# Head attention of a graph network on one core: loops written out, TensorE's steps regrouped in twos, a weight ring of six, VectorE's masks one slot later

## The chip, the cores and the metric

One core of one Trainium2 chip (trn2) runs the whole kernel. The metric is the device time of one execution in microseconds (us); lower is better. The kernel before takes 3810.34 us, the median of three runs.

## The reference, cut to what matters

Four layers work on `x` (8 batches, 2048 nodes, 128 features) with one adjacency matrix `adj` (2048 x 2048): an additive attention, the head attention that is changed here, a neighbour mean, and another additive attention. The change touches layer 1 only, and of it the part between the projections and the output product:

```python
h = maximum(layernorm(x), 0)
q = (h @ W_q).reshape(8, 2048, 4, 32).transpose(0, 2, 1, 3)   # k and v alike
scores = einsum('bhnd,bhmd->bhnm', q, k) / sqrt(32)
scores = where(adj == 0, -inf, scores)
attn = softmax(scores, axis=-1)
out = einsum('bhnm,bhmd->bhnd', attn, v)
x = x + out.transpose(0, 2, 1, 3).reshape(8, 2048, 128) @ W_o + b_o
```

So there are 8 x 4 softmaxes over 2048 x 2048 masked scores.

## The kernel before, in words

`build` runs the stages one after the other, each a block of five engine programs. `nodes1` leaves q and k (float16, a high and a low part) and v in memory, `head_attention` (lines 1046 to 1330) leaves the weighted sums and their denominators, `nodes2` divides and goes on.

`head_attention` treats the four heads of a batch as two units `u` of two heads `a`. A **chunk** is one unit and 512 query nodes (`BANK`), so a batch has `CHUNKS` = 8 and the stage has 64. A **step** `g` is one tile of 128 key nodes (`jt`, 16 of them) of a chunk, for both heads: 128 steps a batch (`BODY`), 1024 in all. In a step:

- **scores**: TensorE makes two matmuls (97 x 128 by 97 x 512, L1231), one for each head, into the two banks of `sc_ps` (`SB` = 2). Row 96 of `qs` holds minus the row's maximum (the "shift"), so no score can overflow. The second head's scores of step g use the bank that the second head's exponential of step g - 1 reads.
- **exponential**: ScalarE, L1314, one instruction for each head, into slot `g % PB` of the ring `w` (`PB` = 4).
- **mask**: `w` is multiplied by 0 or 1 in place: by GpSimd (L1327) in three steps of four, by VectorE (L1276, `mask`) in the steps with `g % 4 == 1` (`mine`).
- **sums**: `weigh(g - LAG)`, with `LAG` = 3: two float32 matmuls (128 x 33 by 128 x 512, L1205) that add into `o_ps`. The profile shows each as two passes, so a step of sums is 4 matmuls.

The shift of a chunk must be known before its scores. So two chunks ahead TensorE also computes plain scores of the same rows with the high parts only, as **slots**: a chunk has 16 of them, one a step (`slot`, L1189), each a pair of 32-row matmuls of the two heads. They go to a ring `mx_ps` of `MB` = 2 slots, and VectorE reads each with two instructions (L1263: add the mask's bias, take the maximum). A slot may be written only when VectorE has taken the one two before it:

```python
pe.wait_ge(mx_taken, SLOTS * chunk + k + 1)      # mx_taken starts at MB + 1
```

After the 16th slot VectorE reduces the maxima (L1270). In step 4 of the next chunk a seventeenth slot, TensorE's transpose of these maxima (L1184), is taken by VectorE (L1252), and SyncE carries the result through memory into row 96 of `qs` (`place_shift`).

An engine executes in program order, and what orders the engines is a set of counting semaphores. TensorE's order in a step is slot, scores, scores, sums of three steps before. Step 4 has the transpose ahead of its scores and its own slot behind its sums. VectorE's order is the mask of step g - 1 where there is one, then the slot of step g.

The batches are a hardware loop (`Fori(0, B)`) in each of the five programs. At a body's end TensorE runs the three sums that are still due, ScalarE copies the last rows out (`keep_rows`), and SyncE has issued loads for a following batch, in the last round too (batch 0 again, `following`). The slots of "two chunks ahead" are run in the last round as well, and nobody uses them.

Of the kernel before, what the change touches and what calls it, by code (L numbers as in the profile page):

```python
# [18 lines left out]
B = 8  # L19
N = 2048  # L20
F = 128
T = N // P
# [1016 lines left out]
def head_attention(nc, io, keep):  # L1039
# [17 lines left out]
    PB, LAG = 4, 3  # L1057
    SB, MB = 2, 2
    mine = [g for g in range(BODY) if g % 4 == 1]
    with ExitStack() as stack:  # L1060
# [50 lines left out]

        def ring(k, chunk_parity):

            return (k + chunk_parity) % MB
# [13 lines left out]
        @block.sync  # L1128
        def _(sp):
            load(sp, 0, 0)  # L1130
            for t in range(T):
                sp.dma_start(mbias[:, t, :], io["mask_bias"][t * P:(t + 1) * P, :]).then_inc(
                    mbias_early if t < 2 * RT else mbias_loaded, 16)
            load_v(sp, 0, 0)
            load(sp, 0, 1)
            load_v(sp, 0, 1)
            place_shift(sp, 0, 0, 0)

            def store(b, c):

                sp.wait_ge(o_kept, 2 * CH * b + c + 1 + 2)
                u, rows = c // CH, slice(c % CH * BANK, (c % CH + 1) * BANK)
                for a in range(2):
                    head = 2 * u + a
                    sp.dma_start(io["heads_t"][bass.ds(b, 1), head * HD:(head + 1) * HD, rows].rearrange("one p n -> p (one n)"),
                                 oe[2 * HD * a:2 * HD * a + HD, c % 2, :]).then_inc(o_stored[c % 2], 16)
                    sp.dma_start(io["sums"][bass.ds(b, 1), head:head + 1, rows].rearrange("one p n -> p (one n)"),
                                 oe[2 * HD * a + HD:2 * HD * a + HD + 1, c % 2, :]).then_inc(o_stored[c % 2], 16)

            with sp.Fori(0, B) as b:  # L1150
                following = (b + 1) % B
                for c in range(CHUNKS):
                    if c == CH:
                        sp.wait_ge(scored, 2 * (BODY * b + STEPS))
                        load(sp, following, 0)
                    if c >= 1:
                        store(b, c - 1)
                    place_shift(sp, CHUNKS * b + c + 1, (c + 1) % CHUNKS // CH, (c + 1) % CH)
                    if c == CH:
                        sp.wait_ge(weighed, BODY * b + STEPS + PB)  # L1160
                        load_v(sp, following, 0)
                sp.wait_ge(scored, 2 * BODY * (b + 1))
                load(sp, following, 1)
                store(b, CHUNKS - 1)
                sp.wait_ge(weighed, BODY * (b + 1) + PB)
                load_v(sp, following, 1)
            for u in range(2):
                sp.wait_ge(qk_loaded[u], LOADS * (B + 1))
                sp.wait_ge(v_loaded[u], 16 * (B + 1))
                sp.wait_ge(o_stored[u], 64 * CH * B)  # L1170
            sp.wait_ge(shift_placed, 32 * (CHUNKS * B + 1))

        @block.tensor
        def _(pe):
            def slot(k, chunk, u, c, first=False):

                n, buf = slots(first)[k], ring(k, c % 2)
                if n < 0 and first:
                    return
# [13 lines left out]
            def weigh(g, i):  # L1193
# [10 lines left out]
                for a in range(2):  # L1204
                    mm = nc.tensor.matmul(o_ps[2 * HD * a:2 * HD * a + HD + 1, c % 2, :], v[u][:, jt, a, :], w[:, g % PB, a, :],  # L1205
                                          start=(jt == 0), stop=(jt == T - 1))
# [9 lines left out]
            with pe.Fori(0, B) as i:  # L1216
                for g in range(BODY):
# [3 lines left out]
                    if jt == 0 and tc == 0:  # L1221
                        pe.wait_ge(qk_loaded[tu], LOADS * (i + on + 1))
                    mine_now = of_step(jt)
                    slot(mine_now[0], CHUNKS * i + g // T + 2, tu, tc)
# [9 lines left out]
                    if g >= LAG:  # L1234
                        weigh(g - LAG, i)
                    for k in mine_now[1:]:
                        slot(k, CHUNKS * i + g // T + 2, tu, tc)
                for g in range(BODY - LAG, BODY):
                    weigh(g, i)

        @block.vector
        def _(dve):
            def slot(k, chunk, c, parity, masks, first=False):

                n, buf = slots(first)[k], ring(k, c % 2)
                if n < 0 and first:
                    return
# [8 lines left out]
                else:  # L1256
                    if not isinstance(due, int):
                        dve.compute_val(due)
# [13 lines left out]
            def mask(g, i):  # L1272
                if g in mine:
                    c, jt = g // T % CH, g % T
                    dve.wait_ge(exp_done, 2 * (BODY * i + g + 1) + SB)
                    nc.vector.tensor_tensor(w[:, g % PB], w[:, g % PB],  # L1276
# [10 lines left out]
            with dve.Fori(0, B) as i:  # L1287
                for g in range(BODY):
                    if g >= 1:
                        mask(g - 1, i)  # L1290
                    for k in of_step(g % T):
                        slot(k, CHUNKS * i + g // T + 2, target(g // T)[2], g // T % 2, (mbias_loaded, 16 * (T - 2 * RT)))
                mask(BODY - 1, i)

        @block.scalar
        def _(act):
# [11 lines left out]
            with act.Fori(0, B) as i:  # L1308
                for g in range(BODY):
                    act.wait_ge(weighed, BODY * i + g + 1)  # L1310
                    for a in range(2):
                        n = 2 * g + a
                        act.wait_ge(scored, 2 * BODY * i + n + 1)
                        nc.scalar.activation(w[:, g % PB, a], sc_ps[:, n % SB], ACT.Exp, scale=SCALE).then_inc(exp_done, 1)  # L1314
                    if g >= T + LAG and (g - LAG) % T == 0:
                        keep_rows((g - LAG) // T - 1, i)
                keep_rows(2 * CH - 1, i)

        @block.gpsimd
        def _(pool):  # L1320
            with pool.Fori(0, B) as i:
                for g in range(BODY):
# [4 lines left out]
                    nc.gpsimd.tensor_tensor(w[:, g % PB], w[:, g % PB],  # L1327
# [653 lines left out]
```

## Time and profile before

| | |
|---|---|
| time, median of 3 runs (lowest, highest) | 3810.34 us (3809.37, 3810.83) |
| the profiled execution's own time | 3810.15 us |
| its span, first to last instruction | 3808.4 us |
| TensorE busy over the span | 3485.4 us (92%) |
| VectorE, ScalarE, GpSimd busy | 3143.4, 1725.5, 1775.2 us |
| mean granted TensorE clock | 0.948 |
| scores of head attention, first to last start | 926.7 to 2869.2 us |

The span lies 1.75 us under the time of the same execution. Times in the rows below are microseconds from the span's start, so they can be laid against each other between engines. TensorE's matmuls are pipelined and their ends are modelled, so the gaps between starts tell what a matmul costs, not the durations.

### The profile page before, as it was taken

The numbers are of one execution on the slowest core, as the hardware profiler recorded it, in microseconds if no ns is written. First come the engines' busy times: TensorE is split into PE (matmuls) and PEld (weight loads), VectorE is DVE, ScalarE is ACT, GpSimd is POOL, SyncE is SP. The second block draws the span as 40 slices with busy tenths as digits, with TensorE's granted clock in tenths as the row PEclk, the third lists the DMA queues.
The fourth block names the chain that finished last, engine by engine and source line by source line (L and its number), as shares of the span: only waits on it lengthen the run. The fifth ranks groups of instructions, "written<-read, shape, count | busy, mean of one in ns | idle before, by whom it ended". The sixth has DMA issues, their size and how long they took to land. (4 is left out here: it accounts for less than half of the span.)

```text
span 3808.4 us, 69809 instructions
## 1 busy us (share of the span) xinstructions
PE 3485.4 (92%) x21189; PEld 1824.9 (48%) x21204; DVE 3143.4 (83%) x7168; ACT 1725.5 (45%) x3546; POOL 1775.2 (47%) x828
## 2 busy tenths in 40 slices
PE   5769999674999999999999999999996999699999
PEld 4659999550111111111111111111114999599999
DVE  6768888667998989989899899898996776477777
ACT  7811111361665656656556566565662544210100
POOL 2300000111887878878888888887882111000000
PEclk8779999895999999999999999999997999899999
DMA  6422121264001110111001110111003332221220
GB/s 238 176 106 79 58 84 57 110 235 157 9 25 28 29 28 5 28 28 28 24 10 29 28 28 6 28 28 28 22 13 109 115 112 79 84 85 51 84 77 36
DMA packets 61261, 245.77 MB, mean 65 GB/s; under 512 B 12130, under 2 KB 14564, under 8 KB 46692
## 3 DMA queue, kind: packets, MB, share of 16 engines
q1 hardware_dynamic: 60900, 241.14, 18.5%
q8 instruction: 204, 3.34, 0.4%
q14 instruction: 157, 1.29, 0.1%
HBM read 156.03 MB, written 85.07 MB: 63 GB/s over the span
## 5 line engine op out<-in xcount | busy, mean ns | idle before, releaser
L1327 POOL TENSOR_TENSOR a_w<-a_w,keep_mask_t 128x1024 f32<-128x1024 f32 x768 | 1635.5, 2155 | 406.1 <-ACT a_w L1314 406.1
L1263 DVE CUSTOM_DVE_ANT_0 a_mx_ps<-a_mx_ps,a_mbias 128x512 f32<-128x512 f32 x2112 | 1389.6, 719 | 143.0 <-PE a_mx_ps L1189 128.8
L1314 ACT ACTIVATE a_w<-a_sc_ps 128x512 f32<-128x512 f32 x2048 | 1111.4, 595 | 813.9 <-PE a_sc_ps L1231 812.5
L1205 PE MATMUL a_o_ps<-a_w,a_v 128*33 128x512 f32 x4096 | 1084.7, 609 | 5.7 <-POOL a_w L1327 5.7
L839 PE MATMUL g_acc<-g_hv,g_w 128*128 128x129 f32 x8192 | 923.8, 276 | 37.0 <-DVE g_w L776 24.5
L839 PEld LDWEIGHTS g_acc<-g_hv,g_w 128*128 128x128 f32 x8192 | 922.3, 193 | 38.7 <-DVE g_w L776 38.7
L776 DVE SCALAR_TENSOR_TENSOR g_w<-g_row,keep_s,keep_mask_t 128x1024 f32<-128x1024 f32 x512 | 647.2, 1282 | 203.5 <-PE g_acc L839 183.6
L1231 PE MATMUL a_sc_ps<-a_qs,a_ks 97*128 97x512 f16 x2048 | 635.2, 393 | 0.0
L1189 PEld LDWEIGHTS a_mx_ps<-a_ks,a_qs 32*128 32x128 f16 x2112 | 94.8, 91 | 895.1 <-DVE a_mx L1263 467.9
L1189 PE MATMUL a_mx_ps<-a_ks,a_qs 32*128 32x512 f16 x2112 | 411.8, 397 | 76.7 <-DVE a_mx L1263 34.2
L1276 DVE TENSOR_TENSOR a_w<-a_w,keep_mask_t 128x1024 f32<-128x1024 f32 x256 | 459.9, 1796 | 1.0
L1205 PEld LDWEIGHTS a_o_ps<-a_w,a_v 128*33 128x33 f32 x4096 | 151.4, 109 | 449.2 <-issue 288.2
L1263 DVE DVE_READ_ACCUMULATOR2_ANT a_mx<- 128x1 f32 x2112 | 289.0, 137 | 0.0
L101 POOL TENSOR_TENSOR p_rstd<-p_tmp,p_minus_half 128x16 f32<-128x16 f32 x24 | 69.6, 2899 | 468.3 <-DVE p_tmp L88 468.3
L1820 PE MATMUL p_sum_ps<-p_g,keep_mask_t 128*128 128x256 f16 x2048 | 243.3, 274 | 1.4 <-issue 1.0
L1231 PEld LDWEIGHTS a_sc_ps<-a_qs,a_ks 97*128 97x128 f16 x2048 | 125.9, 98 | 241.8 <-issue 202.2
L919 POOL MEMSET p_minus_half<- 128x16 f32 x1 | 0.1, 117 | 493.0 <-POOLq L664 493.0
L1820 PEld LDWEIGHTS p_sum_ps<-p_g,keep_mask_t 128*128 128x128 bf16 x2048 | 201.2, 98 | 28.5 <-issue 1.3
L794 ACT COPY g_value<-keep_s 128x16 f32 (+1 forms) x16 | 3.3, 204 | 435.8 <-DMA g_h<-h_nodes 435.8
L803 ACT ACTIVATE g_e<-g_y 128x1024 f32<-128x1024 f32 x16 | 16.9, 1058 | 329.5 <-DVE g_y L741 329.5
L1537 DVE SCALAR_TENSOR_TENSOR p_x<-p_sum_ps,keep_rdeg,p_own 128x128 f32<-128x128 f32 x128 | 44.4, 347 | 72.2 <-PE p_sum_ps L1820 71.6
L1303 ACT COPY a_oe<-a_o_ps 33x512 f32<-33x512 f32 x128 | 73.6, 575 | 29.6 <-PE a_o_ps L1205 28.8
(198 smaller groups left out, 2130.4 us busy)
## 6 DMA issues: line engine op xcount, KB each, us to landing
h_nodes<-p_h SPq DMA_DIRECT2D x16, 1032.0 KB, 3.9
g_h<-h_nodes SPq DMA_DIRECT2D x16, 1032.0 KB, 6.0
p_adj_in<-in_adj SPq DMA_DIRECT2D x16, 1024.0 KB, 8.5
g_row<-u_rows SPq DMA_DIRECT2D x32, 512.0 KB, 7.2
p_x<-x SPq DMA_DIRECT2D x16, 1024.0 KB, 8.5
a_v<-v SPq DMA_DIRECT2D x18, 528.0 KB, 3.8
a_ks<-k_hi SPq DMA_DIRECT2D x72, 128.0 KB, 2.8
a_qs<-q_hi SPq DMA_DIRECT2D x72, 128.0 KB, 2.9
```

What stands on the lines that cost most here:

```text
L101: nc.gpsimd.tensor_tensor(rstd, tmp[:, 3, :], minus_half, ALU.pow).then_inc(rooted, 1)
L776: nc.vector.scalar_tensor_tensor(out=w[:, g % PB, :], in0=row[:, k, cols], scalar=keep["s2_08"][:, bass.ds(b, 1), jt], in1=keep["mask_t"][ ...
L839: mm = nc.tensor.matmul(tile(half, it), w[:, g % PB, it * P:(it + 1) * P], hv[:, k, jt, :], start=(jt == 0 and it % 3 == 0), stop=(jt == T ...
L1189: mm = nc.tensor.matmul(mx_ps[:, buf, a, :], qs[u][a][hi, t * P:(t + 1) * P], ks[u][a][hi, kc * BANK:(kc + 1) * BANK], start=True, stop=True)
L1205: mm = nc.tensor.matmul(o_ps[2 * HD * a:2 * HD * a + HD + 1, c % 2, :], v[u][:, jt, a, :], w[:, g % PB, a, :], start=(jt == 0), stop=(jt = ...
L1231: nc.tensor.matmul(sc_ps[:, n % SB, :], ks[u][a][:, jt * P:(jt + 1) * P], qs[u][a][:, c * BANK:(c + 1) * BANK], start=True, stop=True).the ...
L1263: last = nc.vector.tensor_tensor_reduce(out=mx_ps[:, buf, a, :], in0=mx_ps[:, buf, a, :], in1=mbias[:, t, kc * BANK:(kc + 1) * BANK], scal ...
L1276: nc.vector.tensor_tensor(w[:, g % PB], w[:, g % PB], keep["mask_t"][:, jt, c * BANK:(c + 1) * BANK].unsqueeze(1).to_broadcast([P, 2, BANK ...
L1303: ins = nc.scalar.copy(oe[rows, c % 2, :], o_ps[rows, c % 2, :])
L1314: nc.scalar.activation(w[:, g % PB, a], sc_ps[:, n % SB], ACT.Exp, scale=SCALE).then_inc(exp_done, 1)
L1327: nc.gpsimd.tensor_tensor(w[:, g % PB], w[:, g % PB], keep["mask_t"][:, jt, c * BANK:(c + 1) * BANK].unsqueeze(1).to_broadcast([P, 2, BANK ...
L1820: mm = nc.tensor.matmul(sum_ps[:, it % 2, 0:2 * F], keep["mask_t"][:, jt, it * P:(it + 1) * P], g[k][:, jt].rearrange("p two f -> p (two f ...
```

## The change

- `PB` goes from 4 to 6, and the ring's index counts over all steps, `(BODY * i + g) % PB`, since 128 is no multiple of 6.
- The loop over batches becomes a Python loop in all five programs. The sums due at a body's end are carried into the next batch, as is the last `keep_rows` and the last `store`.
- TensorE handles two steps at a time: for an even g the two slots of g and g + 1, the scores of g, the sums of g - 4 and g - 3, and then the scores of g + 1. In the round that starts at step 4 the transpose and one slot come first, and the third slot stands behind the sums (`late`).
- VectorE takes the slot of step g first and then the mask of g - 1.
- SyncE no longer loads batch 0 again at the end, and `wanted` leaves out the slots beyond the last chunk.

```diff
@@ -1054,7 +1054,7 @@
     UNITS = RT * CH
     TURN = UNITS // 4
     SLOTS = UNITS + 1
-    PB, LAG = 4, 3
+    PB, LAG = 6, 3
     SB, MB = 2, 2
     mine = [g for g in range(BODY) if g % 4 == 1]
     with ExitStack() as stack:
@@ -1109,6 +1109,12 @@
 
             return [k for k, n in enumerate(slots(False)) if (TURN if n < 0 else n) == jt]
 
+        def wanted(n, chunk):
+            return chunk < CHUNKS * B or chunk == CHUNKS * B and n in (-1, *range(TURN))
         def ring(k, chunk_parity):
 
             return (k + chunk_parity) % MB
@@ -1147,35 +1153,36 @@
                     sp.dma_start(io["sums"][bass.ds(b, 1), head:head + 1, rows].rearrange("one p n -> p (one n)"),
                                  oe[2 * HD * a + HD:2 * HD * a + HD + 1, c % 2, :]).then_inc(o_stored[c % 2], 16)
 
-            with sp.Fori(0, B) as b:
-                following = (b + 1) % B
+            for b in range(B):
+                more = b < B - 1
                 for c in range(CHUNKS):
-                    if c == CH:
+                    if c == CH and more:
                         sp.wait_ge(scored, 2 * (BODY * b + STEPS))
-                        load(sp, following, 0)
+                        load(sp, b + 1, 0)
                     if c >= 1:
                         store(b, c - 1)
-                    place_shift(sp, CHUNKS * b + c + 1, (c + 1) % CHUNKS // CH, (c + 1) % CH)
-                    if c == CH:
+                    elif b > 0:
+                        store(b - 1, CHUNKS - 1)
+                        sp.wait_ge(weighed, BODY * b + PB)
+                        load_v(sp, b, 1)
+                    if more or c < CHUNKS - 1:
+                        place_shift(sp, CHUNKS * b + c + 1, (c + 1) % CHUNKS // CH, (c + 1) % CH)
+                    if c == CH and more:
                         sp.wait_ge(weighed, BODY * b + STEPS + PB)
-                        load_v(sp, following, 0)
-                sp.wait_ge(scored, 2 * BODY * (b + 1))
-                load(sp, following, 1)
-                store(b, CHUNKS - 1)
-                sp.wait_ge(weighed, BODY * (b + 1) + PB)
-                load_v(sp, following, 1)
+                        load_v(sp, b + 1, 0)
+                if more:
+                    sp.wait_ge(scored, 2 * BODY * (b + 1))
+                    load(sp, b + 1, 1)
+            store(B - 1, CHUNKS - 1)
             for u in range(2):
-                sp.wait_ge(qk_loaded[u], LOADS * (B + 1))
-                sp.wait_ge(v_loaded[u], 16 * (B + 1))
                 sp.wait_ge(o_stored[u], 64 * CH * B)
-            sp.wait_ge(shift_placed, 32 * (CHUNKS * B + 1))
 
         @block.tensor
         def _(pe):
             def slot(k, chunk, u, c, first=False):
 
                 n, buf = slots(first)[k], ring(k, c % 2)
-                if n < 0 and first:
+                if n < 0 and first or not wanted(n, chunk):
                     return
                 if n < 0:
                     pe.wait_ge(rows_done, chunk)
@@ -1202,7 +1209,7 @@
                 else:
                     pe.wait_ge(masked_pool, (BODY - len(mine)) * i + g - sum(m < g for m in mine) + 1)
                 for a in range(2):
-                    mm = nc.tensor.matmul(o_ps[2 * HD * a:2 * HD * a + HD + 1, c % 2, :], v[u][:, jt, a, :], w[:, g % PB, a, :],
+                    mm = nc.tensor.matmul(o_ps[2 * HD * a:2 * HD * a + HD + 1, c % 2, :], v[u][:, jt, a, :], w[:, (BODY * i + g) % PB, a, :],
                                           start=(jt == 0), stop=(jt == T - 1))
                 mm.then_inc(weighed, 1)
 
@@ -1213,15 +1220,20 @@
                 for k in range(SLOTS):
                     slot(k, chunk, 0, chunk, chunk == 0)
             pe.wait_ge(units_ready, 4)
-            with pe.Fori(0, B) as i:
+            for i in range(B):
                 for g in range(BODY):
                     u, r = g // STEPS, g % STEPS
                     c, jt = r // T, r % T
                     on, tu, tc = target(g // T)
-                    if jt == 0 and tc == 0:
+                    chunk = CHUNKS * i + g // T + 2
+                    if jt == 0 and tc == 0 and chunk < CHUNKS * B:
                         pe.wait_ge(qk_loaded[tu], LOADS * (i + on + 1))
-                    mine_now = of_step(jt)
-                    slot(mine_now[0], CHUNKS * i + g // T + 2, tu, tc)
+                    late = []
+                    if g % 2 == 0:
+                        due = of_step(jt) + of_step(jt + 1)
+                        for k in due[0:2]:
+                            slot(k, chunk, tu, tc)
+                        late = due[2:]
                     if jt == 0:
                         pe.wait_ge(shift_placed, 32 * (CHUNKS * i + g // T + 1))
                     for a in range(2):
@@ -1231,19 +1243,21 @@
                         nc.tensor.matmul(sc_ps[:, n % SB, :], ks[u][a][:, jt * P:(jt + 1) * P],
                                          qs[u][a][:, c * BANK:(c + 1) * BANK], start=True, stop=True).then_inc(scored, 1)
 
-                    if g >= LAG:
-                        weigh(g - LAG, i)
-                    for k in mine_now[1:]:
-                        slot(k, CHUNKS * i + g // T + 2, tu, tc)
-                for g in range(BODY - LAG, BODY):
-                    weigh(g, i)
+                    if g % 2 == 0:
+                        for n in (BODY * i + g - 4, BODY * i + g - 3):
+                            if n >= 0:
+                                weigh(n % BODY, n // BODY)
+                        for k in late:
+                            slot(k, chunk, tu, tc)
+            for g in range(BODY - 4, BODY):
+                weigh(g, B - 1)
 
         @block.vector
         def _(dve):
             def slot(k, chunk, c, parity, masks, first=False):
 
                 n, buf = slots(first)[k], ring(k, c % 2)
-                if n < 0 and first:
+                if n < 0 and first or not wanted(n, chunk):
                     return
                 due = SLOTS * chunk + k + 1
                 if n < 0:
@@ -1254,8 +1268,6 @@
                     dve.wait_ge(shift_ready, chunk)
                     dve.sem_inc(mx_taken, 1)
                 else:
-                    if not isinstance(due, int):
-                        dve.compute_val(due)
                     dve.wait_ge(*masks)
                     dve.wait_ge(mx_scored, due)
                     t, kc = RT * c + n // CH, n % CH
@@ -1273,7 +1285,7 @@
                 if g in mine:
                     c, jt = g // T % CH, g % T
                     dve.wait_ge(exp_done, 2 * (BODY * i + g + 1) + SB)
-                    nc.vector.tensor_tensor(w[:, g % PB], w[:, g % PB],
+                    nc.vector.tensor_tensor(w[:, (BODY * i + g) % PB], w[:, (BODY * i + g) % PB],
                                             keep["mask_t"][:, jt, c * BANK:(c + 1) * BANK].unsqueeze(1).to_broadcast([P, 2, BANK]),
                                             ALU.mult).then_inc(masked_dve, 1)
 
@@ -1284,12 +1296,12 @@
             for chunk in range(2):
                 for k in range(SLOTS):
                     slot(k, chunk, chunk, chunk, (mbias_early, 16 * 2 * RT), chunk == 0)
-            with dve.Fori(0, B) as i:
+            for i in range(B):
                 for g in range(BODY):
+                    for k in of_step(g % T):
+                        slot(k, CHUNKS * i + g // T + 2, target(g // T)[2], g // T % 2, (mbias_loaded, 16 * (T - 2 * RT)))
                     if g >= 1:
                         mask(g - 1, i)
-                    for k in of_step(g % T):
-                        slot(k, CHUNKS * i + g // T + 2, target(g // T)[2], g // T % 2, (mbias_loaded, 16 * (T - 2 * RT)))
                 mask(BODY - 1, i)
 
         @block.scalar
@@ -1305,26 +1317,28 @@
 
             act.sem_inc(exp_done, SB)
             act.sem_inc(o_kept, 2)
-            with act.Fori(0, B) as i:
+            for i in range(B):
                 for g in range(BODY):
                     act.wait_ge(weighed, BODY * i + g + 1)
                     for a in range(2):
                         n = 2 * g + a
                         act.wait_ge(scored, 2 * BODY * i + n + 1)
-                        nc.scalar.activation(w[:, g % PB, a], sc_ps[:, n % SB], ACT.Exp, scale=SCALE).then_inc(exp_done, 1)
+                        nc.scalar.activation(w[:, (BODY * i + g) % PB, a], sc_ps[:, n % SB], ACT.Exp, scale=SCALE).then_inc(exp_done, 1)
                     if g >= T + LAG and (g - LAG) % T == 0:
                         keep_rows((g - LAG) // T - 1, i)
-                keep_rows(2 * CH - 1, i)
+                    if g == LAG and i > 0:
+                        keep_rows(2 * CH - 1, i - 1)
+            keep_rows(2 * CH - 1, B - 1)
 
         @block.gpsimd
         def _(pool):
-            with pool.Fori(0, B) as i:
+            for i in range(B):
                 for g in range(BODY):
                     if g in mine:
                         continue
                     c, jt = g // T % CH, g % T
                     pool.wait_ge(exp_done, 2 * (BODY * i + g + 1) + SB)
-                    nc.gpsimd.tensor_tensor(w[:, g % PB], w[:, g % PB],
+                    nc.gpsimd.tensor_tensor(w[:, (BODY * i + g) % PB], w[:, (BODY * i + g) % PB],
                                             keep["mask_t"][:, jt, c * BANK:(c + 1) * BANK].unsqueeze(1).to_broadcast([P, 2, BANK]),
                                             ALU.mult).then_inc(masked_pool, 1)
 
```

## Rows read from the trace of the kernel before

**Rows 1.** Windows: busy time of each engine, granted clock, DMA share, GB/s.
```profile
1164.14:1170.95 6.81, 3.07 (x15) 0.49 (x11) 0.82 (x3) 1.16 (x2) 2.13 (x2) 0.82 0.82 235
1170.95:1201.25 30.30, 30.06 (x119) 5.65 (x118) 27.65 (x68) 17.36 (x32) 23.62 (x11) 0.87 0.08 23
1500.00:1529.46 29.46, 29.46 (x131) 5.68 (x131) 28.23 (x71) 18.40 (x35) 25.52 (x13) 1.00 0.02 6
```

**Rows 2.** Tile a_sc_ps: count, duration ns min/median/max, first and last start.
```profile
L1231 PE MATMUL a_sc_ps<-a_qs,a_ks x2048: 377/381/634, 926.7 to 2869.2; 97*128 97x512 f16 x187
```

**Rows 3.** Timeline of a plain step: start, duration, engine, line, operation, count.
```profile
1502.70 0.39 PE L1189 MATMUL a_mx_ps<-a_ks,a_qs 32*128 32x512 f16 x2
1502.77 6.30 POOL L1327 TENSOR_TENSOR a_w<-a_w,keep_mask_t 128x1024 f32<-128x1024 f32 x3 [0.97 <-ACT a_w L1314]
...
1503.02 0.60 PE L1231 MATMUL a_sc_ps<-a_qs,a_ks 97*128 97x512 f16 x2
...
1503.45 1.09 ACT L1314 ACTIVATE a_w<-a_sc_ps 128x512 f32<-128x512 f32 x2 [0.76 <-PE a_sc_ps L1231]
...
1503.56 1.05 PE L1205 MATMUL a_o_ps<-a_w,a_v 128*33 128x512 f32 x4
...
1504.55 0.39 PE L1189 MATMUL a_mx_ps<-a_ks,a_qs 32*128 32x512 f16 x2
```

**Rows 4.** Timelines of GpSimd and TensorE at a batch's end.
```profile
1162.05 4.22 POOL L1327 TENSOR_TENSOR a_w<-a_w,keep_mask_t 128x1024 f32<-128x1024 f32 x2 [0.97 <-ACT a_w L1314]
...
1162.31 0.60 PE L1231 MATMUL a_sc_ps<-a_qs,a_ks 97*128 97x512 f16 x2
1162.84 2.77 PE L1205 MATMUL a_o_ps<-a_w,a_v 128*33 128x512 f32 x12
1166.33 1.05 PE L1205 MATMUL a_o_ps<-a_w,a_v 128*33 128x512 f32 x4 [0.72 <-POOL a_w L1327]
1170.41 0.61 PE L1189 MATMUL a_mx_ps<-a_ks,a_qs 32*128 32x512 f16 x2 [3.02 <-issue]
1170.95 1.03 PE L1231 MATMUL a_sc_ps<-a_qs,a_ks 97*128 97x512 f16 x2
1171.91 0.61 PE L1189 MATMUL a_mx_ps<-a_ks,a_qs 32*128 32x512 f16 x2
```

**Rows 5.** Timeline after a transpose: two slots in a row, VectorE idle before them.
```profile
1513.53 0.60 PE L1189 MATMUL a_mx_ps<-a_ks,a_qs 32*128 32x512 f16 x4
1514.07 0.60 PE L1231 MATMUL a_sc_ps<-a_qs,a_ks 97*128 97x512 f16 x2
1514.07 0.70 DVE L1263 CUSTOM_DVE_ANT_0 a_mx_ps<-a_mx_ps,a_mbias 128x512 f32<-128x512 f32 x1 [1.17 <-PE a_mx_ps L1189]
```

**Rows 6.** Timeline ahead of the steps: TensorE waits for VectorE's slots.
```profile
886.47 0.73 DVE L1263 CUSTOM_DVE_ANT_0 a_mx_ps<-a_mx_ps,a_mbias 128x512 f32<-128x512 f32 x1
887.12 0.73 DVE L1263 CUSTOM_DVE_ANT_0 a_mx_ps<-a_mx_ps,a_mbias 128x512 f32<-128x512 f32 x1
887.32 0.61 PE L1189 MATMUL a_mx_ps<-a_ks,a_qs 32*128 32x512 f16 x2 [0.69 <-DVE a_mx L1263]
```

**Rows 7.** Timelines of VectorE and GpSimd around two masks of VectorE.
```profile
1506.94 2.13 POOL L1327 TENSOR_TENSOR a_w<-a_w,keep_mask_t 128x1024 f32<-128x1024 f32 x1
1508.30 1.85 DVE L1276 TENSOR_TENSOR a_w<-a_w,keep_mask_t 128x1024 f32<-128x1024 f32 x1
...
1516.63 1.22 DVE L1276 TENSOR_TENSOR a_w<-a_w,keep_mask_t 128x1024 f32<-128x1024 f32 x1
1517.50 2.34 POOL L1327 TENSOR_TENSOR a_w<-a_w,keep_mask_t 128x1024 f32<-128x1024 f32 x1 [1.06 <-ACT a_w L1314]
1517.77 0.69 DVE L1263 CUSTOM_DVE_ANT_0 a_mx_ps<-a_mx_ps,a_mbias 128x512 f32<-128x512 f32 x1
```

**Rows 8.** Timeline of SyncE at the stage's end.
```profile
2877.39 0.37 SPq L1095 DMA_DIRECT2D a_v<-v  x1
```

## The prediction

> **What bounds the kernel now.** I read the windows first, then the tile of the scores, then the timeline of single steps. Head attention is half of the time: its scores start from 926.7 to 2869.2 us [rows 2]. A chunk of 16 steps takes 29.46 us with TensorE busy throughout and the clock at full speed [rows 1], so 1.84 us a step. The timeline says of what: from slot to scores 0.32, from scores to sums 0.54, from sums to the next slot 0.98 to 0.99 [rows 3]. No wait lies between these, so TensorE sets the pace. VectorE is busy 28.23 of 29.46 us, GpSimd 25.52: both are close behind.
>
> GpSimd and VectorE are tied together. A mask of VectorE that has GpSimd to itself at first takes 1.22 us. One that starts 1.36 us into an operation of GpSimd takes 1.85: GpSimd's ends at 1509.07 and the mask at 1510.15, 1.08 later. And GpSimd's operation that starts inside a mask takes 2.34 for 2.13, ending 1.99 us after the mask [rows 7]. So whoever comes second does its work after the other. The Trainium skill states this as a rule (SBUF — State Buffer, section SBUF: two separate sides): the pair of ports is an exclusive lock, held for a whole instruction by whoever starts first. By that rule, the trace agrees; it would matter most for a mask that starts just behind a GpSimd operation, which is a rival below.
>
> At a batch's end the rhythm breaks: scores at 1162.31, then again at 1170.95 [rows 4], 8.64 us for 1.84, and the next chunk takes 30.30 us at a mean clock of 0.87 [rows 1].
>
> **The loops written out.** The scores' starts cover 1942.3 us for 1023 steps [rows 2]; at 1.841 these would be 1883.6. Of the excess of 58.7, seven batch ends take 7 x 6.80 = 47.6, and 11.1 is left for the eight starts, 1.4 each. The change keeps one start: 57.3 us go. Within a batch the 128 steps are already straight code and run without a gap, so I expect no new cost from more of it. If code loading ate the whole gain, the sum would lack 57; if it costs nothing, it stands. I take nothing.
>
> **What TensorE would save.** Two slots in a row and the scores after them take 0.54 [rows 5] where two single ones take 0.64. A step of sums takes 0.98 alone; three steps in a row have 12 passes in 2.77 against 4 in 1.05 [rows 3, 4], so 0.86 for each further step, and two take 1.84. A round of two steps is then pair 0.54, scores 0.54, sums 1.84, scores and the change to the slots. The last is in no row: between 0.45 (as if the change were free, twice 0.23 from the x2 forms) and 0.63 (a change twice as dear as scores to sums). I take 0.54 as from scores to sums. That makes 3.46 for 3.68, or 27.7 us a chunk, if nothing waits.
>
> **What waits.** The ring of slots still has two places, and now both are written together. The second slot of a round, B, needs VectorE to be done with B of the round before, while the slots that VectorE could do meanwhile are not there yet. Prices for VectorE: it starts a slot 0.54 after TensorE does (1513.53, 1514.07) [rows 5]; its two instructions start 0.65 apart, so a slot is 1.30; TensorE writes the next 0.85 after the slot's second instruction started (886.47, 887.32) [rows 6]; a free mask holds it 1.14 (1516.63, 1517.77) [rows 7].
>
> Let 0 be the start of slot A in a round with g = 4k + 2, in which VectorE's new order is A, mask, B. VectorE starts A at 0.54 and the mask at 1.84. That mask is of step 4k + 1, whose scores started at -0.54; its exponentials start 0.43 later and take 1.09 [rows 3], so it is ready at 0.98. B starts at 2.98, its second instruction at 3.63, and TensorE may write B of the following round at 4.48. TensorE comes there at 3.46 + 0.23 = 3.69, so it waits about 0.8 us (some 0.3 less, since scores of the round at 0 already wait a little for exponentials, which changes nothing in this chain). Everything behind it waits too: from B to scores 0.31, to sums 0.54, to the odd scores 1.84, to the next A 0.54, together 3.23. The next A at g = 4k + 6 stands at 7.71. VectorE has done its two slots by 4.28 + 2.60 = 6.88 and idles until 8.25. So four steps take 7.71 instead of 7.36: TensorE's 3.23 and VectorE's 4.48 now follow one another instead of overlapping, and the wait costs more than the grouping saves.
>
> Is the mask free? In this frame the second head's scores of step 4k + 2 wait for the exponential that ends at 0.98, start at 1.04, and its own exponential ends at 2.07 (0.43 and 0.60 later). GpSimd's next mask starts there at the earliest; VectorE's starts at 1.84, ahead of it. GpSimd's three then run behind it: 2.91 to 4.90 (the 1.99 above), to 7.0 and to 9.1, and VectorE's next mask starts at 7.71 + 1.84 = 9.55. It is free by 0.2 on one side and 0.4 on the other, so I take 1.14.
>
> **The round with the transpose.** Its pair is the transpose and a slot; the third slot goes behind the sums. With x the time at which the pair's second is written: scores x + 0.31, sums x + 0.85, late slot x + 2.69, odd scores x + 3.00, next A x + 3.54. VectorE gets the late slot at x + 3.23 and is done at x + 4.53, later than A could start (x + 4.08). Then A 1.30, mask 1.14, B's first 0.65, release 0.85: x + 8.47. So 0.76 more than 7.71, once a chunk.
>
> A chunk: 3 x 7.71 + 8.47 = 31.60 us for 29.46. Over 64 chunks +137 us.
>
> **The rest.** The skipped slots: in the last two chunks rounds run without slots. There the second head's scores wait for an exponential: 0.43 + 1.09 + 0.06 (GpSimd's end at 1166.27 to TensorE's start at 1166.33 [rows 4] as such a delay) = 1.58, sums 0.31 later, 1.84 for them: 3.73 a round, 29.8 a chunk, so about 3 us less in all. SyncE ends the stage with a load of v issued at 2877.39 [rows 8], behind stores that alone will be left: 1.5 us less (at least 0.5, at most 4, from the loads ahead of them). The ring of six: step g's exponential needs the sums of g - 6, which lie in the round before, so it never waits; with four places it would. The last copy of a batch and its store move to step 3 of the next one. Behind them on SyncE stand a load of v for the second unit and the shift of chunk 1, which is needed 10 steps later: hidden behind some 19 us; without this cover its few us would fall on TensorE eight times. On ScalarE the copies still lie between exponentials as in every other chunk. GpSimd's masks are used a round later than before; by the frame above the third ends at 9.1 and its sums are due after 12.
>
> Sum, from the profiled execution's 3810.15 (0.2 under the median of the runs): + 137 - 57.3 - 3 - 1.5 = 3885 us.
>
> **Rivals.**
> 1. Faster: B's wait doesn't bind. The place is TensorE's wait for VectorE in the rounds without a mask. For it: VectorE's work for four steps, 4 x 1.30 + 1.14 = 6.34, is under TensorE's 6.92, so only the order is against it. Then GpSimd's lockstep with the masks is the floor: three operations 6.30 [rows 3] and 1.08 for the mask, less 0.14 of overlap, 7.24 for four steps, 29.0 a chunk: -30 - 62 gives 3719; at the old 29.46 it is 3748. It decides at a chunk of 30.43, where 64 x 0.97 equals the 62 gained elsewhere, that is at a period of 7.42: 0.29 less than my 7.71, in a chain of nine terms of which one is assumed. Against it: the other eight are read.
> 2. The mask loses the race to GpSimd. It starts 0.2 us ahead; if GpSimd's operation were first, the mask would end at 2.07 + 2.12 + 1.08 = 5.27, the period become 2.2 longer, 9.9, and the time about 4450. By the skill's rule above the same: the loser waits for the whole operation. It decides where the mask starts later than GpSimd's operation. If only some chunks lose it, the time is in between.
> 3. The grouping does what I say and unrolling gives nothing back, because straight code has to be fetched: 3885 + 57 = 3942.
> 4. TensorE's waits of 0.8 us in 7.7 lower its clock. At the lower level (1.2 GHz) slot to scores takes 0.54 and scores to slot 0.96 [rows 4]; with sums at twice their time a round is about 6.5, and the stage over 1000 us longer. Against it: where it fell, at a batch's end, TensorE had stood still for 3.02 us [rows 4]; the gaps to come are a quarter of that.
>
> **How the numbers follow.** My forecast has 0.72, with a range of its own of 3850 to 3925: the unread change from scores to slots gives 0.09 x 4 x 64 = 23 each way, and 0.05 in the handovers of the chain 13 more. Rival 1 has 0.12, rival 2 0.06, rival 3 0.04, rival 4 0.02; 0.04 is for a wait that binds in part only and ends near the old time. The range of 3825 to 3955 holds my case nearly whole, rival 3, and part of the last. Faster by over 0.2% (7.6 us, about what a measurement of this kernel can tell from no change) 0.13, within it 0.03, slower 0.84.
>
> **What the profile after would show.** No gaps at 1164 to 1171 or their like; chunks of 31.6 us; TensorE idle before L1189 in every second round, released by VectorE, 0.5 to 0.8 us, and VectorE idle about 1.4 us every four steps, released by TensorE; all masks of VectorE near 1.22 us. Two sums in a row at 1.84, and the odd scores to the slot at 0.54. I am wrong if chunks stay under 30.4 us, or if masks of over 3 us appear.

## The result and the profile after

The changed kernel takes 3873.3 us (median of 4 runs, 3871.8 to 3880.7) against 3810.6 before, a ratio of 1.0166 with a 95% interval of 1.0149 to 1.0184: 63 us slower. Forecast were 3885, 3825 to 3955. Its profiled execution took 3873.6 us.

The windows view of the kernel after: a chunk that holds a batch's end, the one behind it, and a plain one (columns as in [rows 1]).

```profile
1148.62:1180.27 31.65, 29.49 (x132) 6.80 (x131) 26.50 (x71) 18.47 (x35) 27.61 (x14) 1.00 0.03 7
1180.27:1211.65 31.38, 29.40 (x130) 6.67 (x130) 26.00 (x71) 18.32 (x34) 27.11 (x13) 1.00 0.26 71
1499.00:1530.40 31.40, 29.41 (x131) 6.77 (x129) 26.25 (x71) 18.40 (x36) 27.37 (x12) 1.00 0.02 5
```

A plain chunk takes 31.40 us for the 29.46 of [rows 1], and now TensorE has 2 us without work in it and VectorE 5. The end of a batch costs 0.25 us where it cost 6.8. The clock stays at 1.00 through the waits.

The timelines of TensorE and VectorE over four steps of the kernel after, from one slot A behind which a mask stands to the next such one (VectorE's next wait is its last line):

```profile
1521.16 0.60 PE L1196 MATMUL a_mx_ps<-a_ks,a_qs 32*128 32x512 f16 x4
1521.76 0.88 PE L1243 MATMUL a_sc_ps<-a_qs,a_ks 97*128 97x512 f16 x2
1522.57 1.91 PE L1212 MATMUL a_o_ps<-a_w,a_v 128*33 128x512 f32 x8
1524.41 0.60 PE L1243 MATMUL a_sc_ps<-a_qs,a_ks 97*128 97x512 f16 x2
1524.95 0.39 PE L1196 MATMUL a_mx_ps<-a_ks,a_qs 32*128 32x512 f16 x2
1525.56 0.39 PE L1196 MATMUL a_mx_ps<-a_ks,a_qs 32*128 32x512 f16 x2 [0.22 <-DVE a_mx L1275]
1525.88 0.61 PE L1243 MATMUL a_sc_ps<-a_qs,a_ks 97*128 97x512 f16 x2
1526.41 1.91 PE L1212 MATMUL a_o_ps<-a_w,a_v 128*33 128x512 f32 x8
1528.26 0.61 PE L1243 MATMUL a_sc_ps<-a_qs,a_ks 97*128 97x512 f16 x2
1528.80 0.60 PE L1196 MATMUL a_mx_ps<-a_ks,a_qs 32*128 32x512 f16 x4
```

```profile
1521.70 0.70 DVE L1275 CUSTOM_DVE_ANT_0 a_mx_ps<-a_mx_ps,a_mbias 128x512 f32<-128x512 f32 x1 [1.14 <-PE a_mx_ps L1196]
1522.32 0.73 DVE L1275 CUSTOM_DVE_ANT_0 a_mx_ps<-a_mx_ps,a_mbias 128x512 f32<-128x512 f32 x1
1522.96 1.22 DVE L1288 TENSOR_TENSOR a_w<-a_w,keep_mask_t 128x1024 f32<-128x1024 f32 x1
1524.10 0.69 DVE L1275 CUSTOM_DVE_ANT_0 a_mx_ps<-a_mx_ps,a_mbias 128x512 f32<-128x512 f32 x1
1524.71 0.73 DVE L1275 CUSTOM_DVE_ANT_0 a_mx_ps<-a_mx_ps,a_mbias 128x512 f32<-128x512 f32 x1
1529.34 0.70 DVE L1275 CUSTOM_DVE_ANT_0 a_mx_ps<-a_mx_ps,a_mbias 128x512 f32<-128x512 f32 x1 [0.98 <-PE a_mx_ps L1196]
```

From 1521.16 to 1528.80 are 7.64 us for four steps. Read the chain across the two engines: slot A written at 1521.16, VectorE at it at 1521.70, the mask at 1522.96, slot B at 1524.10 and 1524.71, and only then, 0.85 later, TensorE's B at 1525.56. TensorE had written the A before it at 1524.95 and could have gone on 0.23 later, so it waited 0.38. Then 3.24 to the next A at 1528.80, for which VectorE has idled 0.98; before the A at 1521.16 it had idled 1.14. I had put about 1.4.

### The profile page after: what moved, and what is told of

Read it like the earlier page. It is cut to its first block and busy times, and to the rows that moved or that the text cites. A ratio compares the mean times of both kernels' runs of the same rounds, so it can differ in the third digit from the quotient of the medians.

```text
span 3871.4 us, 60296 instructions
## 1 busy us (share of the span) xinstructions
PE 3449.7 (89%) x21147; PEld 1885.7 (49%) x21147; DVE 2980.8 (77%) x7053; ACT 1724.5 (45%) x3546; POOL 1887.0 (49%) x828
## 5 line engine op out<-in xcount | busy, mean ns | idle before, releaser
L1341 POOL TENSOR_TENSOR a_w<-a_w,keep_mask_t 128x1024 f32<-128x1024 f32 x768 | 1748.1, 2297 | 362.3 <-ACT a_w L1326 359.3
L1275 DVE CUSTOM_DVE_ANT_0 a_mx_ps<-a_mx_ps,a_mbias 128x512 f32<-128x512 f32 x2056 | 1368.9, 718 | 333.9 <-PE a_mx_ps L1196 314.3
L1212 PE MATMUL a_o_ps<-a_w,a_v 128*33 128x512 f32 x4096 | 980.4, 599 | 0.5 <-POOL a_w L1341 0.5
L1243 PE MATMUL a_sc_ps<-a_qs,a_ks 97*128 97x512 f16 x2048 | 663.8, 387 | 29.8 <-ACT a_w L1326 9.9
L1196 PE MATMUL a_mx_ps<-a_ks,a_qs 32*128 32x512 f16 x2056 | 374.5, 391 | 156.7 <-DVE a_mx L1275 133.7
L1243 PEld LDWEIGHTS a_sc_ps<-a_qs,a_ks 97*128 97x128 f16 x2048 | 150.6, 96 | 676.6 <-ACT a_w L1326 422.3
L1212 PEld LDWEIGHTS a_o_ps<-a_w,a_v 128*33 128x33 f32 x4096 | 195.2, 110 | 461.1 <-issue 364.9
L1288 DVE TENSOR_TENSOR a_w<-a_w,keep_mask_t 128x1024 f32<-128x1024 f32 x256 | 314.5, 1229 | 40.2 <-ACT a_w L1326 40.2
L1196 PEld LDWEIGHTS a_mx_ps<-a_ks,a_qs 32*128 32x128 f16 x2056 | 82.7, 91 | 508.2 <-DVE a_mx L1275 323.4
L1729 ACT ACTIVATE p_hn<-p_x,p_shift,p_rstd 128x128 f32<-128x128 f32 x128 | 50.1, 479 | 68.1 <-DVE p_shift L94 68.1
```

What stands on the lines that cost most here:

```text
L1196: mm = nc.tensor.matmul(mx_ps[:, buf, a, :], qs[u][a][hi, t * P:(t + 1) * P], ks[u][a][hi, kc * BANK:(kc + 1) * BANK], start=True, stop=True)
L1243: nc.tensor.matmul(sc_ps[:, n % SB, :], ks[u][a][:, jt * P:(jt + 1) * P], qs[u][a][:, c * BANK:(c + 1) * BANK], start=True, stop=True).the ...
L1275: last = nc.vector.tensor_tensor_reduce(out=mx_ps[:, buf, a, :], in0=mx_ps[:, buf, a, :], in1=mbias[:, t, kc * BANK:(kc + 1) * BANK], scal ...
L1288: nc.vector.tensor_tensor(w[:, (BODY * i + g) % PB], w[:, (BODY * i + g) % PB], keep["mask_t"][:, jt, c * BANK:(c + 1) * BANK].unsqueeze(1 ...
L1341: nc.gpsimd.tensor_tensor(w[:, (BODY * i + g) % PB], w[:, (BODY * i + g) % PB], keep["mask_t"][:, jt, c * BANK:(c + 1) * BANK].unsqueeze(1 ...
L1729: ins = nc.scalar.activation(hn[:, t, :], x3[k][:, t, :], ACT.Relu, bias=shift3[:, t:t + 1], scale=rstd3[:, t:t + 1])
```

## The experiments

The kernel before, timed again beside them, had medians of 3810.2, 3808.5 and 3811.4 us. Experiments 1, 5, 9 and 10 have several runs; the others have a single one, so no interval. "Chunk" is the median distance of the first scores of two chunks. The diffs are shortened, and where words stand in them they stand for the lines they name.

**1. The loops alone.** The code of the kernel after, with these parts as before:

```diff
-    PB, LAG = 6, 3
+    PB, LAG = 4, 3
@@ TensorE, each step
-                    if g % 2 == 0: two slots; sums of g - 4 and g - 3; third slot
+                    slot(due[0]); scores; weigh of BODY * i + g - LAG; slots of due[1:]
@@ VectorE
+                    mask(g - 1, i) ahead of the slots of step g
```

> Of the change only the loops written out (with the carried sums, the skipped slots and the shorter end); TensorE's order in single steps, VectorE's mask ahead of its slot and the ring of four as before. Theory: the batch ends cost 57.3 us, nothing else moves, chunks stay at 29.46 us: 3810.6 - 57.3 - 1.5 - 1 = 3751 us. Rival (straight code has to be fetched and costs what the loop ends cost): 3810 us, with idle time of all engines at places that are no batch ends.

Measured: 3748.9 us, 0.9837 of before (0.9823 to 0.9850). The timeline of this kernel at its first batch's end (1168.51 is step 0 of the next batch):

```profile
1166.67 0.60 PE L1239 MATMUL a_sc_ps<-a_qs,a_ks 97*128 97x512 f16 x2
1167.21 1.05 PE L1212 MATMUL a_o_ps<-a_w,a_v 128*33 128x512 f32 x4
1168.19 0.39 PE L1196 MATMUL a_mx_ps<-a_ks,a_qs 32*128 32x512 f16 x2
1168.51 0.61 PE L1239 MATMUL a_sc_ps<-a_qs,a_ks 97*128 97x512 f16 x2
```

A step of 1.84 as anywhere else, and all seven chunks that hold a batch's end take 29.46. So the loops, with the skipped slots and the shorter end, are worth 61 us (put at 60), straight code costs next to nothing here, and the rest of the change loses 124. (In both timings of this kernel the same five chunks, none with a batch's end, are 0.2 to 0.3 us longer, 1.4 in all; the kernel before has none such. Whether that is a cost of straight code was not tried.)

**2. VectorE's mask, placed first again.**

```diff
@@ VectorE, on the kernel after
+                    if g >= 1: mask(g - 1, i)
                     for k in of_step(g % T): slot(k, ...)
-                    if g >= 1: mask(g - 1, i)
```

> The changed kernel with VectorE's mask ahead of the slot again. Theory (TensorE's 3.2 us and VectorE's time from slot A to the release of B follow one another): the mask now waits for its exponentials, 1.05 us after slot A is written, so A starts at 2.19 instead of 0.54 + mask 1.14 behind it; B's release comes 0.5 us later in four steps: chunk 33.4 for 31.4 us, about 4000 us. Rival (where the mask stands doesn't matter, only the sum of VectorE's work): 3873 us.

Measured: 3999.4 us, chunk 33.41. The order of VectorE's work counts by the microsecond, since it lies in the chain. This kernel's timeline has the mask waiting for its exponentials while slot A lies ready:

```profile
1504.72 1.23 DVE L1288 TENSOR_TENSOR a_w<-a_w,keep_mask_t 128x1024 f32<-128x1024 f32 x1 [1.50 <-ACT a_w L1326]
```

Slot A was written at 1503.66 and VectorE starts it at 1505.87, 2.21 later, for the 2.19 expected. So with slots in twos the later mask is the better one.

**3. The later mask with single steps.** As 1, but with the ring of six and with VectorE's slot ahead of its mask.

> Loops written out, ring of six, TensorE's order in single steps as before, but VectorE's mask one slot later as in the change. Theory (whoever of GpSimd and VectorE comes second waits for the other's whole instruction): every fourth mask now comes just behind a GpSimd operation and takes about 2.8 us, the others 1.22; sums wait for it; chunk 30.3 to 30.4, about 3807 us. Rival (a mask never takes over 2.2 us, later is better or the same): 3751 us.

Measured: 3815.3 us, chunk 30.49, both a little above what I gave (3807, 30.3 to 30.4); 66 of the 256 masks take over 2.6 us, 187 take 1.22. One of each from the timeline of VectorE, and GpSimd's operations at the dear one:

```profile
1514.66 1.22 DVE L1283 TENSOR_TENSOR a_w<-a_w,keep_mask_t 128x1024 f32<-128x1024 f32 x1
1522.93 2.79 DVE L1283 TENSOR_TENSOR a_w<-a_w,keep_mask_t 128x1024 f32<-128x1024 f32 x1
```

```profile
1522.51 7.29 POOL L1336 TENSOR_TENSOR a_w<-a_w,keep_mask_t 128x1024 f32<-128x1024 f32 x3 [0.46 <-ACT a_w L1321]
```

The mask starts 0.42 us behind GpSimd's, whose operation of 2.12 ends at 1524.63; the mask ends at 1525.72, 1.09 later. It waited for all that was left. The three GpSimd operations take 7.29 for the 6.30 of [rows 3], as they wait for the mask in their turn. So the same move gains 2.0 us a chunk with slots in twos (experiment 2), and with single ones the chunk is 1.0 longer than in experiment 1. The ring of six differs there too, and it was not run alone; but the waits of the dear masks account for the direction.

**4. VectorE's masks left out.**

```diff
@@ on the kernel after: TensorE
-                    pe.wait_ge(masked_dve, len(mine) * i + mine.index(g) + 1)
+                    pe.wait_ge(exp_done, 2 * (BODY * i + g + 1) + SB)
@@ VectorE: no mask at all
```

> The changed kernel with VectorE's 256 masks left out (a quarter of the steps is summed unmasked). Theory 1 (once VectorE's release no longer binds, the round is bound by the exponentials: the second head's scores 1.58 us after the odd scores, 0.31 to the sums, 1.84 for them, so 3.73 a round, and 0.76 more in the transpose's chunk round): chunk 30.6 to 30.9, about 3830 us. Theory 2 (TensorE alone is the bound then, 3.46 a round): chunk 28 to 28.5, about 3670 us. Rival (VectorE's masks have nothing to do with it): 3873 us.

Measured: 3870.2 us, chunk 31.23. None of the three names this number well: theory 1 has the mechanism and is 0.3 to 0.6 us a chunk and 40 us in all short, and the rival has the time. This kernel's timeline of TensorE tells what holds it; its first line is the slot behind the transpose's round:

```profile
1508.38 0.39 PE L1196 MATMUL a_mx_ps<-a_ks,a_qs 32*128 32x512 f16 x2 [0.76 <-DVE a_mx L1275]
...
1511.62 0.60 PE L1196 MATMUL a_mx_ps<-a_ks,a_qs 32*128 32x512 f16 x4
1512.22 0.88 PE L1243 MATMUL a_sc_ps<-a_qs,a_ks 97*128 97x512 f16 x2
1513.03 1.91 PE L1212 MATMUL a_o_ps<-a_w,a_v 128*33 128x512 f32 x8
1514.87 0.60 PE L1243 MATMUL a_sc_ps<-a_qs,a_ks 97*128 97x512 f16 x2
1515.41 0.60 PE L1196 MATMUL a_mx_ps<-a_ks,a_qs 32*128 32x512 f16 x4
```

Two slots are four matmuls in a row, so B does not wait, but for once a chunk, behind the transpose's round (0.76 us). And the even scores take 0.88 for 0.60: the second head's wait for their bank, as 1.14 us lie between the odd scores and these. A round is 3.79 us, where I had put 3.73, and 3.79 is more than the 3.68 of two steps before. Eight of these are 30.32, and the transpose adds 0.91 where I had put 0.76. There are two walls at nearly the same place, 7.64 and 7.58 for four steps, so taking one away shows little. The next two experiments part them.

**5 and 6. Only the slots in twos, with and without VectorE's masks.**

```diff
@@ TensorE, on the kernel after: slot, slot, scores, sums, scores, sums
-                    if g % 2 == 0:
-                        for n in (BODY * i + g - 4, BODY * i + g - 3): weigh, then the third slot
+                    n = BODY * i + g - 4
+                    if n >= 0: weigh(n % BODY, n // BODY); then the third slot
```

> The changed kernel with only the slots written in twos: the round is slot, slot, scores, sums, scores, sums, so no two sums in a row and no scores that wait for exponentials. Theory (two slots together behind a ring of two make TensorE's part after B and VectorE's part up to B's release follow one another: from B 0.32 to scores, 0.53 to sums, 0.98, 0.54, 0.98 to the next slot A, 3.35 in all, then 4.40 on VectorE's side, or 7.7 for four steps): chunk 31.3 to 31.6 us, about 3873 us as the changed kernel. Rival (the pairs of sums and the exponentials they make the scores wait for are the cause): chunk 28.7 to 29.4 us, 3700 to 3750 us.

> The kernel slots_pair with VectorE's 256 masks left out (a quarter of the steps is summed unmasked). Theory (two walls stand at nearly the same place in the changed kernel, VectorE's release of B and the exponentials behind a pair of sums; here neither is left): TensorE alone is the bound, 7.17 for four steps, chunk 28.8 to 29.0 us, about 3715 us. Rival (something else, common to all kernels with slots in twos, holds the chunk at 31.2): about 3865 us, as the changed kernel without its masks.

Measured: 3869.6 us with the masks (1.0163 of before, 1.0145 to 1.0181; chunk 31.37) and 3712.1 without (chunk 28.94). With the masks, TensorE's timeline has the wait for B four steps apart:

```profile
1512.65 0.39 PE L1196 MATMUL a_mx_ps<-a_ks,a_qs 32*128 32x512 f16 x2 [0.43 <-DVE a_mx L1274]
1520.42 0.39 PE L1196 MATMUL a_mx_ps<-a_ks,a_qs 32*128 32x512 f16 x2 [0.43 <-DVE a_mx L1274]
```

Without the pairs of sums no scores wait for a bank, and the loss is all there still: the ring of two behind slots written in twos, with VectorE's mask between them, makes it without the other wall. That the chunk is so near the 31.40 of the kernel after is in part chance: four steps take 7.76 here, one change of kind more than the 7.64 there, and the four with the transpose 8.08 for 8.39. And here, with the other wall gone, VectorE's 256 masks of 1.22 us are worth 157 us. The timeline of the kernel without them is TensorE's own time for this order, 3.58 a round, of which 0.54 for two slots and the change to scores:

```profile
1503.21 0.60 PE L1196 MATMUL a_mx_ps<-a_ks,a_qs 32*128 32x512 f16 x4
1503.75 0.60 PE L1243 MATMUL a_sc_ps<-a_qs,a_ks 97*128 97x512 f16 x2
1504.29 1.05 PE L1212 MATMUL a_o_ps<-a_w,a_v 128*33 128x512 f32 x4
1505.27 0.60 PE L1243 MATMUL a_sc_ps<-a_qs,a_ks 97*128 97x512 f16 x2
1505.81 1.05 PE L1212 MATMUL a_o_ps<-a_w,a_v 128*33 128x512 f32 x4
1506.79 0.60 PE L1196 MATMUL a_mx_ps<-a_ks,a_qs 32*128 32x512 f16 x4
```

**7. Only the sums in twos.** On the kernel after, the second slot stands behind the sums:

```diff
-                        for k in due[0:2]:
+                        for k in due[0:1]:
                             slot(k, chunk, tu, tc)
-                        late = due[2:]
+                        late = due[1:]
```

> The changed kernel with only the sums in twos: the round is slot, scores, sums, sums, slot, scores. Theory (the odd scores are followed within 0.9 us by the even scores, whose second head waits until 1.58 after the odd scores for its bank, so a round is 1.58 + 0.31 + 1.84 + 0.32 = 4.05 to 4.1 us, and VectorE's mask doesn't matter): chunk 32.6 to 33.3 us, 3950 to 3995 us. Rival (pairs of sums are free and only the slots matter): chunk under 29.5 us, 3750 us.

Measured: 4006.7 us, chunk 33.48. The timeline of TensorE has a round of 4.12 us in it, from the slot at 1499.68 to the one at 1503.80:

```profile
1499.68 0.39 PE L1196 MATMUL a_mx_ps<-a_ks,a_qs 32*128 32x512 f16 x2
1500.01 0.60 PE L1243 MATMUL a_sc_ps<-a_qs,a_ks 97*128 97x512 f16 x2
1500.71 0.39 PE L1196 MATMUL a_mx_ps<-a_ks,a_qs 32*128 32x512 f16 x2
1501.14 0.88 PE L1243 MATMUL a_sc_ps<-a_qs,a_ks 97*128 97x512 f16 x2
1501.95 1.91 PE L1212 MATMUL a_o_ps<-a_w,a_v 128*33 128x512 f32 x8
1503.80 0.39 PE L1196 MATMUL a_mx_ps<-a_ks,a_qs 32*128 32x512 f16 x2
1504.12 0.60 PE L1243 MATMUL a_sc_ps<-a_qs,a_ks 97*128 97x512 f16 x2
```

Odd scores at 1500.01, the next odd ones at 1504.12. The time is 12 us above the range I gave. Six of a chunk's eight rounds take 4.11; the two at the transpose take 4.33 and 4.49, 0.60 more together, and in the second of them TensorE waits for VectorE:

```profile
1509.91 0.39 PE L1196 MATMUL a_mx_ps<-a_ks,a_qs 32*128 32x512 f16 x2 [0.86 <-DVE a_mx L1275]
```

Masks take 2.86 us here on the mean, which I had said wouldn't matter; whether this wait comes of them was not tried.

**8. The mask two slots later.** On the kernel after, `mask(g - 2, i)` for `mask(g - 1, i)`, so behind B.

> The changed kernel with VectorE's mask two slots later, behind B instead of between A and B. Theory (the mask then starts about 3.1 us after A, inside GpSimd's operation that starts at 2.1 to 2.2, waits for its end and for nothing else): masks of 2.2 to 2.7 us for 1.22; the wait falls into VectorE's idle time only in part: chunk 31.6 to 32.0, 3885 to 3910 us. Rival 1 (GpSimd goes on with its next operation first): masks over 4 us and over 4100 us. Rival 2 (masks share the port and take 1.3 to 1.8 us): below 3873 us, since B is released 1.1 us earlier.

Measured: 3914.8 us, chunk 32.03, masks of 2.67 us on the mean, time and chunk just above my ranges. Timelines of VectorE and GpSimd:

```profile
1504.20 2.50 DVE L1288 TENSOR_TENSOR a_w<-a_w,keep_mask_t 128x1024 f32<-128x1024 f32 x1
```

```profile
1503.50 2.12 POOL L1342 TENSOR_TENSOR a_w<-a_w,keep_mask_t 128x1024 f32<-128x1024 f32 x1 [0.57 <-ACT a_w L1327]
1505.88 4.90 POOL L1342 TENSOR_TENSOR a_w<-a_w,keep_mask_t 128x1024 f32<-128x1024 f32 x2 [0.26 <-ACT a_w L1327]
```

GpSimd's operation ends at 1505.62, the mask at 1506.70: 1.08 again. The masks are 1.4 us longer than in the kernel after, and four steps only 0.16: behind B, VectorE's idle time takes up most of such a wait. This does not test rival 2's price of 4450, whose waiting mask stands between A and B, in the chain; no run here has that.

**9 and 10. An order that beats both.** By experiment 6, two slots together cost nothing where no mask of VectorE lies between them. So: rounds of four steps, slots in twos in one half, single in the half with the mask, never two sums in a row, `mine` at `g % 4 == 0`.

```diff
@@ TensorE, ahead of the scores of g
+  g % 4 == 0: the slots of g        g % 4 == 2: the slots of g and g + 1
@@ behind the scores of g
+  g % 4 == 0: the slots of g + 1    then always: the sums of g - 4
```

> All loops written out, ring of six, VectorE's mask one slot on, but in the steps with g % 4 == 0, and TensorE in rounds of four steps: slot, scores, slot, sums, scores, sums, slot, slot, scores, sums, scores, sums. So two slots stand together only once in four steps, in the half without a mask, and no two sums do. Theory (B's wait costs only where VectorE's mask lies between the two slots; then one change of kind less in four steps is worth 0.09 us): four steps 7.27, chunk 29.1 us, about 3725 to 3735 us, just ahead of the kernel with the loops alone. Rival (masks and GpSimd's operations collide more in this order, 28.9 us being their floor): chunk 29.4 to 29.8 us, 3750 to 3770 us.

> The kernel with the loops alone once more, on the same chip as the mixed order, so that the two can be compared: 3749 us.

Measured on one chip, five runs each: 3738.4 us (3732.1 to 3739.3), 0.9805 of before (0.9791 to 0.9818), and 3747.8 (3746.4 to 3750.1), 0.9835 (0.9821 to 0.9848), for the loops alone. The two's runs don't overlap, and 9 us are between their medians. The chunk is 29.25, 0.15 above my figure, and the time 3 us above my range. The mixed kernel also has the ring of six and its masks in other steps and at another place, so the 9 us are those of the bundle.

## Why the prediction was right

The direction, the size and the place came out: +63 us for a forecast of +75.

- **The chain of four steps: right, 7.64 for 7.71.** Term by term: slot to VectorE 0.54 (0.54), slot A 1.26 (1.30), mask 1.14 (1.14), B's first instruction 0.61 (0.65), release 0.85 (0.85), to scores 0.32 (0.31), to sums 0.53 (0.54), the two steps of sums 1.85 (1.84), odd scores and the change to the slots 0.54 (0.54, the one that was in no row). The 0.07 too much is in VectorE's slots: the first instruction after a wait or a mask gives way to the second 0.61 to 0.62 later, and I had taken 0.65 from instructions in a run.
- **The round with the transpose: right, with one term beside it.** From its B at 1501.79 to the next behind a mask at 1510.18 are 8.39 for 8.47, less by the same 0.08 in VectorE's slots. The four steps behind it take 7.74 and not 7.64, since the second head's scores wait for their bank there, which the chain left out. With two fours of 7.64 that makes the chunk's 31.4.
- **The chunks:** 64 x 1.94 = 124 us for 137.
- **The loops: right, 5 us too much.** 57.3 and 3 for the skipped slots were put; from the first step's scores to the last step's are 2010.9 us, where 1023 steps at 31.40 / 16 would be 2007.6. The excess is 3.3, down from 58.7, so 55.4 for 60.3. Chunk by chunk: the first has 2.3 too much (I kept 1.4), the seven with a batch's end 0.25 each, four others 0.23 each, and the skipped slots give 1.6 for my 3, as rounds without slots take 3.79 and not 3.73.
- **The stage's end: low, within its bounds.** The next stage's first transfer is issued 9.7 us after the last scores' start (2937.7 to 2947.43), before 13.5 (2869.2 [rows 2] to 2882.68): 3.8 us for my 1.5, which I had bounded by 0.5 and 4. SyncE's timelines, before and after, and the tile of the scores after:

```profile
2882.68 0.38 SPq L1444 DMA_DIRECT2D p_all_sums<-sums  x1
```

```profile
2947.43 0.35 SPq L1458 DMA_DIRECT2D p_all_sums<-sums  x1
L1243 PE MATMUL a_sc_ps<-a_qs,a_ks x2048: 376/389/634, 926.5 to 2937.7; 97*128 97x512 f16 x187
```

- **The mask's cover: right.** 249 of 256 masks take under 1.3 us, and they start 0.44 us ahead of GpSimd's operation, for the 0.2 I had. Rival 2 did not happen, but its mechanism was shown twice (experiments 3 and 8).
- **TensorE's wait before B: wrong in size.** I expected 0.5 to 0.8 and it is 0.38, because TensorE comes there 3.79 + 0.23 after its A and not 3.46 + 0.23. I wrote of these 0.3 that they change nothing in the chain, and for the chain that holds. But they are a second wall, 7.58, right behind the first.
- **Rival 1 was mispriced for that reason.** Experiment 4 comes nearest to its condition, B's wait not binding, and the time there is 3870 and not 3719, though VectorE's masks are gone besides. I had looked for the next bound in TensorE's own time and in GpSimd's port and had the exponentials' figure in the text without making it a bound. At that price no faster case was left in this order, and my 0.13 for faster was too much.

The 0.25 us at a batch's end are a wait that the kernel before has already (`n + 1 if n else SB`): the first scores of a batch wait for the exponentials of both heads of the step before, all others for one head's alone. In the kernel after that step's scores start only 1.5 us ahead, and TensorE's timeline shows the scores 0.57 behind slot B instead of 0.32:

```profile
1179.67 0.39 PE L1196 MATMUL a_mx_ps<-a_ks,a_qs 32*128 32x512 f16 x2 [0.22 <-DVE a_mx L1275]
1180.24 0.59 PE L1243 MATMUL a_sc_ps<-a_qs,a_ks 97*128 97x512 f16 x2 [0.18 <-ACT a_w L1326]
```

In experiments 4, 7 and 8 it is 0.49; in the kernel with the loops alone, where steps lie 1.84 apart, it is nothing. The kernel without this wait was not run.

What stays open: what VectorE's masks have to do with the 12 us of experiment 7, and the 0.23 of the four other chunks.

## What to carry to other kernels

Grouping like instructions on the busiest engine saves what a change of kind costs (here 0.1 us each) and can ask the rings that it runs past for one more place, which was not run here: with a ring of two and a mask in between, two slots written together turn two engines that overlapped into a chain, and their times add. Price each ring and bank that the new order touches as a loop of its own (writer, reader, release, writer) and compare all of those loops, not only the one you look at: here two of them stood 0.06 us apart. Where a change bundles a sure gain with an order, take them apart before the verdict on either; the loops alone were worth 1.6% and the bundle lost 1.7%.

## What the runs showed of the hardware

A mask of VectorE and one of GpSimd, both of which read and write SBUF, the on-chip memory, never shared. Of two that overlapped, the one that started second ended 1.08 to 1.09 us (VectorE: 192 masks of the kernel before, all 256 of experiment 8) or 1.98 to 2.12 us (GpSimd: 256 operations of the kernel before) after the other's end, also when it started 0.42 us behind. VectorE's first slot instruction after a wait or a mask is followed by the second 0.61 to 0.62 us later, in a run 0.65. TensorE's granted clock was 1.00 over the whole stage of the kernel after (926.5 to 2937.7), in which it stood still for 0.2 to 0.8 us every few us.
